# Preactivated 3x3 convolutions in float32: tiles of one size on TensorE, and row loads issued by ScalarE

## The chip, the cores and the metric

The kernel runs on one core of one Trainium2 chip. The metric is device time in microseconds of one execution, given as the median of several runs.

## The reference

The input `x` is 8 images of 8 channels of 1024 x 1024 float32 values. Two layers follow each other. Each normalises its input over groups of two channels (mean and variance over the group's two whole planes of one image), convolves the result 3x3 with 8 output channels and a padding of one, and adds the bias and the layer's own input.

```python
def _gn(v, G=4, eps=1e-5):
    B_, C_, H_, W_ = v.shape
    g = v.reshape(B_, G, C_ // G, H_, W_)
    m = jnp.mean(g, axis=(2, 3, 4), keepdims=True)
    s = jnp.var(g, axis=(2, 3, 4), keepdims=True)
    return ((g - m) / jnp.sqrt(s + eps)).reshape(v.shape)
...
x = x + _L0_conv_ref(_gn(x), L0_conv_weight, L0_conv_bias)
x = x + _L1_conv_ref(_gn(x), L1_conv_weight, L1_conv_bias)
```

## The kernel before

**Tiling.** The 128 partitions hold 16 image rows of 8 channels each (a block, 512 KB). An image has 64 blocks; two of them make a unit, so that a layer of an image (a pass) has 32 units and the kernel has 16 passes and 512 units. `x_tile` has 8 slots of one block, so four units' worth. The result of a unit is gathered in PSUM (`conv`, two parities of two blocks of 1024 columns, all of PSUM), evicted with the bias by ScalarE into `out_tile` (a ring of four units), and stored by GpSimd: layer 0 to the scratch tensor `mid_dram`, layer 1 to the output. Normalisation is folded into the weights `wts` (the rstd) and the bias, so that the matmuls read `x_tile` as it was loaded; the residual is an identity added to the middle tap.

**Matmuls of a unit.** The three kernel rows are one banded weight matrix over (row, channel), the three kernel columns are three shifts `kw` of the moving rows, and a unit has two halves `c` of 512 columns. A quarter is 32 partitions, four image rows. Its output needs its own rows and some of the quarter above. `whole` makes the odd quarters with four matmuls of 64 rows by 32 columns, `split` makes the even ones with eight matmuls of 32 by 32: the quarter's own rows (L405) and the quarter above (L410), the latter for the other half of the columns, `1 - c`. One `whole` and one `split` are called a round here; a unit has six, in the order of lines 424 to 437. The profile shows two records for each matmul call, since float32 goes through in two passes. After three rounds the wait at L431 asks for the end of the first half, because the second half adds to the same places of PSUM from other rows of the array.

**Order of the work.** SP issues all loads in one queue: the row blocks, and the 1 MB pieces of the next image that VectorE takes statistics of (`load_stat`, 32 for each image, at the units in `STAT_UNITS`). After the matmuls of unit g have ended (`conv_done`) it loads the second block of unit g+3 and the first of unit g+4. ScalarE evicts unit g in three activations. VectorE takes the statistics of `out_tile` in layer 0 (four instructions a unit) and of the next image's pieces. Between two passes VectorE, TensorE and ScalarE work out mean, variance, weights and bias (`sums_of`, `sums`); no matmul of the next pass can start before.

In the rows the matmuls are named by their lines: L395 `whole`, L405 and L410 `split`.

## Time and profile before

| | |
|---|---|
| median of 3 runs | 6538.94 us (6537.51 to 6539.03) |
| the profiled execution's own time | 6541.13 us |
| its span in the trace | 6539.5 us |
| TensorE busy | 6236.9 us (95%), mean granted clock 0.984 |
| ScalarE, VectorE, GpSimd busy | 1711.8, 1424.5, 591.4 us |
| moved by DMA | 1344.60 MB, 206 GB/s over the span |

The span is the time from the first to the last instruction. A share of busy time of TensorE says only that some matmul was in the array; up to sixteen tiles of 32 by 32 can be at work at once, and the share doesn't tell how many were. The granted clock is the part of TensorE's 2.4 GHz that it was given: 1.0 is 2.4 GHz, 0.5 is 1.2 GHz.

### The profile page before, as it was taken

Reading aid. Unit: us, or ns where it says so; the run is one execution under the profiler, and the core shown is the slowest. Engines: PE = TensorE matmul, PEld = TensorE weight load, DVE = VectorE, ACT = ScalarE, POOL = GpSimd, SP = SyncE. Lnnn points to the kernel's source line nnn. Section 1 sums busy time; section 2 is a strip of 40 time slices with the busy share of each in tenths; the row PEclk is TensorE's granted clock in tenths of the full one; section 3 lists DMA queues with packets and bytes.
Section 4 is the critical chain, followed back from the end, with each engine's and each line's share of the span. In section 5 each row is a group of like instructions: output and inputs, shape, how many; then the busy total and the mean of one; then the engine's idle time right before and its main releaser. Section 6 shows DMA issues by size and latency. Waiting matters only on the chain.

```text
span 6539.5 us, 167994 instructions
## 1 busy us (share of the span) xinstructions
PE 6236.9 (95%) x74176; PEld 1052.5 (16%) x74176; DVE 1424.5 (22%) x2460; ACT 1711.8 (26%) x1553; POOL 591.4 (9%) x1059
## 2 busy tenths in 40 slices
PE   2999999999999999999999999999999999999999
PEld 0111111111111111111111111111111111111111
DVE  6332113321133101331113311223012331022100
ACT  0222222222222222222222222222222222222222
POOL 0000010000000000000010000100000000000000
PEclk9999999999999999999999999999999999999999
DMA  7665666756566566766666666666666666655454
GB/s 273 219 215 203 218 191 216 226 202 215 191 218 225 199 214 193 217 205 214 223 186 219 205 221 209 200 215 204 219 206 203 213 206 217 207 162 177 154 172 153
DMA packets 334159, 1344.60 MB, mean 206 GB/s; under 512 B 38800, under 2 KB 38928, under 8 KB 301200
## 3 DMA queue, kind: packets, MB, share of 16 engines
q1 hardware_dynamic: 184688, 805.91, 40.8%
q0 software_dynamic: 147456, 536.94, 21.9%
q14 instruction: 186, 1.52, 0.1%
q10 hardware_dynamic: 1824, 0.14, 0.0%
q8 instruction: 5, 0.08, 0.0%
HBM read 805.45 MB, written 536.87 MB: 205 GB/s over the span
## 4 chain that ended last, share of the span: by engine, by line
PE 95%; DVE 2%; issue 1%; DMA 1%; ACT 1%; SPq 0%; DVEq 0%; ACTq 0%; POOL 0%; POOLq 0%
PE conv L395 47%; PE conv L405 45%; PE conv L410 3%; DMA stat_tile<-x_dram 1%; DVE bn_x L602 1%; DVE mv_mid L490 0%; ACT out_tile L344 0%; ACT out_tile L346 0%; DVE wts L541 0%; DVE bn_mid L476 0%; DVE newton L531 0%; DVE x_tile L556 0%; PE conv L371 0%; PE conv L367 0%; SPq L183 0%
## 5 line engine op out<-in xcount | busy, mean ns | idle before, releaser
L410 PE MATMUL conv<-x_tile,wts 32*32 32x512 f32 x24576 | 3334.1, 602 | 0.0
L405 PE MATMUL conv<-x_tile,wts 32*32 32x512 f32 x24576 | 3334.0, 602 | 0.0
L395 PE MATMUL conv<-x_tile,wts 64*32 64x512 f32 x24576 | 3281.4, 604 | 34.9 <-DVE bias L562 34.9
L342 ACT ACTIVATE out_tile<-conv,bias 128x1024 f32<-128x1024 f32 x512 | 570.6, 1114 | 4619.3 <-PE conv L410 4619.3
L476 DVE BATCH_NORM_STATS2 bn_mid<-out_tile 128x6 f32<-128x512 f32 x1024 | 658.7, 685 | 2241.6 <-ACT out_tile L342 1989.6
L468 DVE BATCH_NORM_STATS2 bn_x<-stat_tile 128x6 f32<-128x512 f32 x896 | 550.6, 679 | 2013.8 <-DMA stat_tile<-x_dram 2013.8
L405 PEld LDWEIGHTS conv<-x_tile,wts 32*32 32x32 f32 x24576 | 530.4, 103 | 2591.3 <-issue 2591.3
L395 PEld LDWEIGHTS conv<-x_tile,wts 64*32 64x32 f32 x24576 | 475.9, 105 | 2612.3 <-issue 2612.3
L346 ACT ACTIVATE out_tile<-conv,bias 64x1024 f32<-64x1024 f32 x512 | 569.3, 1112 | 13.1
L344 ACT ACTIVATE out_tile<-conv,bias 64x1024 f32<-64x1024 f32 x512 | 567.4, 1108 | 13.0
L297 POOL DMA_DIRECT2D mid_dram<-out_tile x512 | 273.8, 535 | 2845.6 <-ACT out_tile L342 2319.2
L297 POOL DMA_DIRECT2D out_dram<-out_tile x512 | 269.0, 525 | 2895.0 <-ACT out_tile L342 2425.9
L410 PEld LDWEIGHTS conv<-x_tile,wts 32*32 32x32 f32 x24576 | 530.4, 103 | 0.0
L367 PE MATMUL conv<-share,average 128*128 128x4 f32 x32 | 7.7, 311 | 183.4 <-DVE share L488 111.0
L497 DVE COPY mean<-conv 128x4 f32<-128x4 f32 x16 | 2.6, 163 | 394.3 <-PE conv L367 394.3
L602 DVE BATCH_NORM_STATS2 bn_x<-stat_tile 128x512 f32 x128 | 78.9, 681 | 24.1 <-DMA stat_tile<-x_dram 23.7
L377 PE MATMUL conv<-taken,plain 64*32 64x1 f32 x384 | 13.5, 190 | 58.0 <-DVE plain L539 58.0
L304 POOL TENSOR_SCALAR pad_row<-zeros,own_mean 8x1024 f32<-8x1024 f32 x16 | 46.0, 2873 | 150.7 <-DVE own_mean L525 120.0
L352 ACT ACTIVATE root<-var 128x4 f32<-128x4 f32 x16 | 3.3, 205 | 134.4 <-DVE var L517 134.3
L367 PEld LDWEIGHTS conv<-share,average 128*128 128x128 f32 x32 | 6.6, 256 | 196.3 <-issue 196.3
L483 DVE BATCH_NORM_AGGREGATE mv_x<-bn_x 128x2 f32<-128x192 f32 x32 | 29.3, 978 | 4.6 <-DVE bn_x L468 4.3
L490 DVE BATCH_NORM_AGGREGATE mv_mid<-bn_mid 128x2 f32<-128x768 f32 x8 | 29.0, 3622 | 1.2 <-DVE bn_mid L476 0.3
(48 smaller groups left out, 123.9 us busy)
## 6 DMA issues: line engine op xcount, KB each, us to landing
stat_tile<-x_dram SPq DMA_DIRECT2D x256, 1024.0 KB, 8.8
mid_dram<-out_tile POOLq DMA_DIRECT2D x512, 512.0 KB, 6.7
out_dram<-out_tile POOLq DMA_DIRECT2D x512, 512.0 KB, 5.3
x_tile<-x_dram SPq DMA_DIRECT2D x504, 512.0 KB, 6.0
x_tile<-mid_dram SPq DMA_DIRECT2D x504, 512.0 KB, 4.3
x_tile<-x_dram SPq DMA_DIRECT2D x8, 480.0 KB, 6.6
x_tile<-mid_dram SPq DMA_DIRECT2D x8, 480.0 KB, 6.4
x_tile<-pad_row SPq DMA_DIRECT2D x16, 32.0 KB
```

The source lines that it names most:

```text
L297: pool.dma_start(to, out_tile[:, g % RING, i]).then_inc(stored[g % RING], 16)
L304: pool.tensor_scalar(pad_row[0:CH, :], zeros[0:CH, :], own_mean[0:CH, 0:1], None, ALU.add).then_inc(pad_row_filled, 1)
L342: act.activation(out_tile[:, slot, 0], conv[:, parity, 0], ACT.Identity, bias=bias[:, 0:1]).then_inc(evicted, 1)
L344: act.activation(out_tile[HALF:P, slot, 1], conv[0:HALF, parity, 1], ACT.Identity, bias=bias[0:HALF, 0:1]).then_inc(evicted, 1)
L346: act.activation(out_tile[0:HALF, slot, 1], conv[HALF:P, parity, 1], ACT.Identity, bias=bias[HALF:P, 0:1]).then_inc(evicted, 1)
L395: nc.tensor.matmul(columns_of(parity, i, 2 * h + 1, c), wts[part, WHOLE, kw], rows_of(HALF * h, HALF, 2 * j + i, c, kw), start=(kw == 0), ...
L405: nc.tensor.matmul(columns_of(parity, i, 2 * h, c), wts[part, SPLIT, kw], rows_of(HALF * h, TILE, slot, c, kw), start=first, stop=end)
L410: last = nc.tensor.matmul(columns_of(parity, i, 2 * h, 1 - c), wts[part, SPLIT, kw], rows_of(TILE * q, TILE, above, 1 - c, kw), start=firs ...
L468: last = dve.bn_stats(bn_x[:, i * STAT_PARTS + q, :], stat_tile[:, s, q * BANK:(q + 1) * BANK])
L476: last = dve.bn_stats(bn_mid[:, (2 * u + i) * HALVES + h, :], out_tile[:, u % RING, i, h * BANK:(h + 1) * BANK])
L483: last = dve.bn_aggr(mv_x[:, g, :], bn_x[:, g * PER_GROUP:(g + 1) * PER_GROUP, :] .rearrange("p a b -> p (a b)"))
L602: last = dve.bn_stats(bn_x[:, bass.ds(k * (STAT_SLOTS * STAT_PARTS) + (s * STAT_PARTS + q), 1), :] .rearrange("p a b -> p (a b)"), stat_ti ...
```

## The change

`whole` and `split` are replaced by one function `add`, in which every matmul has 32 rows by 32 columns: for each of the two blocks of a unit, four for the quarters' own rows (MAIN) and four for the quarters above (ABOVE). A unit has 96 matmul calls in place of 72. The wait on `half_added` stands between the third and the fourth round. The bias matmuls (`sums`) are 24 in place of 12, and the weights, the identity and the table of taps have the forms MAIN and ABOVE.

The row blocks, the pad row and the head row are issued by ScalarE, in `load_next(n, g)` behind the three activations of unit g; the conditions are the same, except that the head row of layer 1 is asked for at unit 4 in place of unit 0. SP keeps the statistics pieces alone; in its loop it waits for the matmuls of the unit before the one at which a piece is due, and for a free slot of `stat_tile`. At the start, ScalarE asks for the first seven blocks behind its table of taps.

```diff
-            def whole(parity, j, c, kw):
-                for i in range(2):
-                    for h in range(2):
-                        part = slice(HALF * h, HALF * (h + 1))
-                        nc.tensor.matmul(columns_of(parity, i, 2 * h + 1, c), wts[part, WHOLE, kw],
-                                         rows_of(HALF * h, HALF, 2 * j + i, c, kw),
-                                         start=(kw == 0), stop=(kw == KW - 1))
-
-            def split(parity, j, c, kw):
+            def add(parity, j, c, kw):
                 first, end = c == 0 and kw == 0, c == 1 and kw == KW - 1
                 for i in range(2):
                     slot = 2 * j + i
-                    for h in range(2):
-                        part = slice(HALF * h, HALF * h + TILE)
-                        nc.tensor.matmul(columns_of(parity, i, 2 * h, c), wts[part, SPLIT, kw],
-                                         rows_of(HALF * h, TILE, slot, c, kw), start=first, stop=end)
-                        q = 1 if h else 3
+                    for q in range(QUARTERS):
                         part = slice(TILE * q, TILE * (q + 1))
-                        above = slot if h else (slot - 1) % SLOTS
-                        last = nc.tensor.matmul(columns_of(parity, i, 2 * h, 1 - c),
-                                                wts[part, SPLIT, kw],
-                                                rows_of(TILE * q, TILE, above, 1 - c, kw),
+                        nc.tensor.matmul(columns_of(parity, i, q, c), wts[part, MAIN, kw],
+                                         rows_of(TILE * q, TILE, slot, c, kw), start=first, stop=end)
+                    for q in range(QUARTERS):
+                        above = (q - 1) % QUARTERS
+                        part = slice(TILE * above, TILE * (above + 1))
+                        last = nc.tensor.matmul(columns_of(parity, i, q, 1 - c), wts[part, ABOVE, kw],
+                                                rows_of(TILE * above, TILE,
+                                                        slot if q else (slot - 1) % SLOTS, 1 - c, kw),
                                                 start=first, stop=end)
                 return last
...
-                whole(parity, j, 0, 0)
-                split(parity, j, 0, 0)
-                whole(parity, j, 0, 1)
-                split(parity, j, 0, 1)
-                whole(parity, j, 0, 2)
-                split(parity, j, 0, 2).then_inc(half_added, 1)
-                whole(parity, j, 1, 0)
+                for kw in range(KW):
+                    last = add(parity, j, 0, kw)
+                last.then_inc(half_added, 1)
                 pe.wait_ge(half_added, UNITS * p + TRIP * t + (j + 1))
                 pe.sem_inc(unit_begun)
-                split(parity, j, 1, 0)
-                whole(parity, j, 1, 1)
-                split(parity, j, 1, 1)
-                whole(parity, j, 1, 2)
-                last = split(parity, j, 1, 2)
+                for kw in range(KW):
+                    last = add(parity, j, 1, kw)
                 last.then_inc(conv_done, 1)
...
+            def load_next(n, g, last_image):
+                layer, u = divmod(g, UNITS)
+                if g == UNITS:
+                    for s in range(RING):
+                        act.wait_ge(stored[s], stores_before(n, UNITS + s))
+                        act.sem_inc(rows_asked)
...
+                if layer == 0 and u == RING:
+                    act.wait_ge(stored[0], stores_before(n, RING))
+                    act.sem_inc(rows_asked)
+                    load_head(1, n)
...
+                if (g + TRIP - 1) % UNITS == UNITS - 1:
+                    load_last_pad(layer, n)
+                    load(TRIP, 0)
+                    act.wait_ge(last_pad_loaded, 32 * n + 16 * (layer + 1))
+                    act.sem_inc(rows_asked)
+                    load(TRIP - 1, 1)
+                else:
+                    load(TRIP - 1, 1)
+                    load(TRIP, 0)
...
                                bias=bias[HALF:P, 0:1]).then_inc(evicted, 1)
-
-            def image(n, first_image):
+                load_next(n, g, last_image)
...
-            def image(n, last_image):
-                for g in range(2 * UNITS):
...
+            def image(n):
+                for i in range(STATS):
+
+                    sp.wait_ge(conv_done, units_through(n, STAT_UNITS[i] - 1) if STAT_UNITS[i] else
+                               2 * UNITS * n + 1)
                     sp.sem_inc(rows_wanted)
+                    load_stat(n + 1, i, STATS * n + (STATS + i + 1 - STAT_SLOTS))
```

On TensorE, the start of a unit read before like this (the matmuls of the first round and of half the second):

```order
L395 MATMUL conv<-x_tile,wts 32x512 x4
L405 MATMUL conv<-x_tile,wts 32x512
L410 MATMUL conv<-x_tile,wts 32x512
L405 MATMUL conv<-x_tile,wts 32x512
L410 MATMUL conv<-x_tile,wts 32x512
L405 MATMUL conv<-x_tile,wts 32x512
L410 MATMUL conv<-x_tile,wts 32x512
L405 MATMUL conv<-x_tile,wts 32x512
L410 MATMUL conv<-x_tile,wts 32x512
L395 MATMUL conv<-x_tile,wts 32x512 x4
```

And now, from the second round of a unit to the wait in its middle (here L390 is MAIN and L395 is ABOVE):

```order
L390 MATMUL conv<-x_tile,wts 32x512 x4
L395 MATMUL conv<-x_tile,wts 32x512 x4
L390 MATMUL conv<-x_tile,wts 32x512 x4
L395 MATMUL conv<-x_tile,wts 32x512 x4
L412 REGISTER_ALU
L390 MATMUL conv<-x_tile,wts 32x512 [waits half_added]
L390 MATMUL conv<-x_tile,wts 32x512 x3
L395 MATMUL conv<-x_tile,wts 32x512 x4
```

The tiles of 64 rows are gone, and the wait has a whole round of 32 by 32 matmuls ahead of it whose end it needs; before, the four matmuls of a `whole` stood between.

On ScalarE two evictions in the middle of layer 0 read before:

```order
L342 ACTIVATE out_tile<-conv,bias 128x1024 [waits mid_taken,stored1,conv_done]
L344 ACTIVATE out_tile<-conv,bias 64x1024
L346 ACTIVATE out_tile<-conv,bias 64x1024
L342 ACTIVATE out_tile<-conv,bias 128x1024 [waits mid_taken,stored2,conv_done]
L344 ACTIVATE out_tile<-conv,bias 64x1024
L346 ACTIVATE out_tile<-conv,bias 64x1024
```

And now, at unit 28 of layer 0, where the pad row is asked for as well:

```order
L329 ACTIVATE out_tile<-conv,bias 128x1024 [waits mid_taken,stored0,conv_done]
L331 ACTIVATE out_tile<-conv,bias 64x1024
L333 ACTIVATE out_tile<-conv,bias 64x1024
L282 DMA x_tile<-pad_row 8x1024 [waits stored0,stored1,stored2,stored3,pad_row_filled]
L273 DMA x_tile<-mid_dram 128x1024
L273 DMA x_tile<-x_dram 120x1x1024 [waits last_pad_loaded]
L329 ACTIVATE out_tile<-conv,bias 128x1024 [waits mid_taken,stored1,conv_done]
L331 ACTIVATE out_tile<-conv,bias 64x1024
L333 ACTIVATE out_tile<-conv,bias 64x1024
L273 DMA x_tile<-mid_dram 128x1024 x2
```

Each eviction is followed by two loads, and at unit 28 the next eviction stands behind a wait for the pad row's landing.

## Rows read from the trace of the kernel before

**Rows 1.** The page: the span, and TensorE's busy time.

```profile
span 6539.5 us, 167994 instructions
...
PE 6236.9 (95%) x74176; PEld 1052.5 (16%) x74176; DVE 1424.5 (22%) x2460; ACT 1711.8 (26%) x1553; POOL 591.4 (9%) x1059
```

**Rows 2.** The page: the chain that ended last, by line.

```profile
PE conv L395 47%; PE conv L405 45%; PE conv L410 3%; DMA stat_tile<-x_dram 1%; DVE bn_x L602 1%; DVE mv_mid L490 0%; ACT out_tile L344 0%; ACT out_tile L346 0%; DVE wts L541 0%; DVE bn_mid L476 0%; DVE newton L531 0%; DVE x_tile L556 0%; PE conv L371 0%; PE conv L367 0%; SPq L183 0%
```

**Rows 3.** Timeline, one round: start, duration (us), engine, line, instructions.

```profile
3011.06 1.06 PE L395 MATMUL conv<-x_tile,wts 64*32 64x512 f32 x8
...
3012.05 0.10 PEld L405 LDWEIGHTS conv<-x_tile,wts 32*32 32x32 f32 x1 [0.84 <-issue]
3012.05 0.61 PE L405 MATMUL conv<-x_tile,wts 32*32 32x512 f32 x1
...
3012.51 0.59 PE L405 MATMUL conv<-x_tile,wts 32*32 32x512 f32 x1
...
3012.55 0.59 PE L410 MATMUL conv<-x_tile,wts 32*32 32x512 f32 x1
3013.07 0.15 PEld L395 LDWEIGHTS conv<-x_tile,wts 64*32 64x32 f32 x8 [0.84 <-issue]
```

**Rows 4.** Waits: who waited for what, us in total, times, longest.

```profile
PEld conv L395 <- issue: 2612.3, 3072, 2.6
PEld conv L405 <- issue: 2591.3, 3072, 1.7
```

**Rows 5.** Timeline of ScalarE, one eviction and the next one's start.

```profile
3019.28 1.11 ACT L342 ACTIVATE out_tile<-conv,bias 128x1024 f32<-128x1024 f32 x1 [8.68 <-PE conv L410]
...
3021.55 1.11 ACT L346 ACTIVATE out_tile<-conv,bias 64x1024 f32<-64x1024 f32 x1
3031.35 1.11 ACT L342 ACTIVATE out_tile<-conv,bias 128x1024 f32<-128x1024 f32 x1 [8.68 <-PE conv L410]
```

**Rows 6.** The page: DMA queues (q1 SP, q0 GpSimd): packets, MB, share.

```profile
q1 hardware_dynamic: 184688, 805.91, 40.8%
q0 software_dynamic: 147456, 536.94, 21.9%
```

**Rows 7.** Windows: busy us by engine, then granted clock, DMA share, GB/s.

```profile
82.00:92.00 10.00, 0.00 (x0) 0.00 (x0) 2.38 (x4) 0.00 (x0) 0.00 (x0) 1.00 1.04 242
110.00:150.00 40.00, 32.38 (x368) 6.65 (x370) 10.80 (x31) 6.88 (x7) 4.75 (x4) 1.00 0.24 68
516.00:528.00 12.00, 4.21 (x44) 2.23 (x52) 9.73 (x30) 0.20 (x1) 2.90 (x1) 0.50 0.23 93
546.00:550.00 4.00, 4.00 (x56) 0.67 (x48) 0.00 (x0) 0.00 (x0) 0.00 (x0) 1.00 1.00 405
948.00:956.00 8.00, 8.00 (x112) 1.33 (x96) 2.57 (x4) 3.33 (x3) 1.07 (x2) 1.00 0.97 256
```

**Rows 8.** The issue line of the row loads: duration ns min/median/max, and landing.

```profile
L183 SPq DMA_DIRECT2D x_tile<-x_dram x512: 536/540/970, 73.5 to 6090.2; - x171
L183 SPq DMA_DIRECT2D x_tile<-mid_dram x512: 327/333/438, 473.5 to 6495.8; - x171
...
DMA to landing us min/median/max: 3.2/4.7/19.6
```

**Rows 9.** Timeline of TensorE around the end of layer 0 of image 0.

```profile
505.90 1.06 PE L395 MATMUL conv<-x_tile,wts 64*32 64x512 f32 x8
...
525.75 1.93 PE L395 MATMUL conv<-x_tile,wts 64*32 64x512 f32 x8 [2.51 <-DVE bias L562]
...
529.49 1.08 PE L395 MATMUL conv<-x_tile,wts 64*32 64x512 f32 x4
```

**Rows 10.** Timeline of ScalarE at the end of image 0.

```profile
914.21 1.11 ACT L342 ACTIVATE out_tile<-conv,bias 128x1024 f32<-128x1024 f32 x1 [8.68 <-PE conv L410]
```

**Rows 11.** Timeline of TensorE at the start of image 1.

```profile
922.48 1.93 PE L395 MATMUL conv<-x_tile,wts 64*32 64x512 f32 x8 [1.78 <-DVE bias L562]
```

More of the change, by code:

```diff
@@ L37 @@
 PASSES = 2 * IMAGES
-WHOLE, SPLIT = range(2)
+MAIN, ABOVE = range(2)
+QUARTERS = P // TILE
 HALVES = SIDE // BANK
@@ new lines, in rows_of, with load_block @@
+            def rows_of(layer, n, first, rows):
+                if layer == 0:
+                    return x_by_row[first:first + rows, bass.ds(n, 1)].rearrange("r n c w -> r (n c) w")
+                return mid[bass.ds(n, 1), CH * first:CH * (first + rows), :] \
+                    .rearrange("n a w -> (n a) w")
+            def load_block(layer, n, b):
+                first = ROWS * b + 1
+                rows = ROWS - 1 if b == BLOCKS - 1 else ROWS
+                act.dma_start(x_tile[0:CH * rows, b % SLOTS, 1:SIDE + 1],
+                             rows_of(layer, n, first, rows)).then_inc(rows_loaded[b % SLOTS], 16)
@@ L354, in image @@
                     for u in range(UNITS):
-                        evict(n, layer * UNITS + u, first_image)
-            image(0, True)
-            with act.Fori(1, IMAGES) as n:
-                image(n, False)
+                        evict(n, layer * UNITS + u, first_image, last_image)
+            load_head(0, 0)
+            for b in range(LAST_SLOT):
+                load_block(0, 0, b)
+            image(0, first_image=True)
+            with act.Fori(1, IMAGES - 1) as n:
+                image(n)
+            image(IMAGES - 1, last_image=True)
         @block.tensor
@@ L374, in sums @@
                 pe.sem_inc(unit_begun)
-                for j in range(P // TILE):
-                    for kw in range(KW):
-                        last = nc.tensor.matmul(
-                            conv[TILE * j:TILE * (j + 1), 0, 0, GROUPS:GROUPS + 1],
-                            plain[0:HALF, kw], taken[0:HALF, :],
-                            start=(kw == 0), stop=(kw == KW - 1))
+                for j in range(QUARTERS):
+                    for kind in (MAIN, ABOVE):
+                        for kw in range(KW):
+                            last = nc.tensor.matmul(
+                                conv[TILE * j:TILE * (j + 1), 0, 0, GROUPS:GROUPS + 1],
+                                plain[0:TILE, kind, kw], taken[0:TILE, :],
+                                start=(kind == MAIN and kw == 0), stop=(kind == ABOVE and kw == KW - 1))
                 last.then_inc(bias_summed, 1)
@@ L538, in make_weights @@
                 wait_for_all()
[L539 removed]
+                dve.tensor_scalar(plain[:, :, :, :], band[:, layer], own_rstd[:, 0:1], None,
                                   ALU.mult).then_inc(taken_known, 1)
```

122 lines of the change are left out of this document (38 added, 84 removed).

## The prediction

> **What bounds the kernel now.** I read the page first: TensorE has a matmul in flight for 6236.9 of 6539.5 us [rows 1], and the chain that ended last is its conv matmuls for 95% [rows 2]. So the time is TensorE's, but a busy share doesn't say how full the array was. For that I took the timeline of one round [rows 3]. Eight records of `whole` start at 3011.06 and run 1.06 us. The first of `split` starts at 3012.05, when they are through, and the next `whole` at 3013.07: a round takes 2.01 us, 0.99 for `whole` and 1.02 for `split`, one behind the other. Inside `split` eight matmuls of different tiles start together, and the second pass of each 0.46 us after the first (3012.05, 3012.51). By `columns_of`, `whole` writes column quarters 1 and 3 from all 128 rows, `split` quarters 0 and 2 from all rows: the two halves of a round use different halves of the array and still don't overlap. What the reader is to see is the idle time of the weight loads: 0.84 us ahead of each `whole` and of each `split` [rows 3], 3072 times each, that is six times in each of 512 units, 2612.3 and 2591.3 us in all [rows 4]. Within a kind the weights are loaded while other matmuls run; across the kinds nothing is loaded ahead, though the tiles wanted are free. A unit takes six rounds, 12.07 us from one eviction to the next [rows 5]; 512 of them are 6180 us, and the other 360 us are the start (some 118 us: of 110 to 150 TensorE is busy for 32.38 [rows 7]) and the changes of pass.
>
> The second reading is of DMA, since it comes next. The two queues' packets take 40.8% and 21.9% of 16 engines' span [rows 6]: 62.7% of 6539.5 us are **4100 us of transfers** if the engines never idled. At a full share the rate depends on what is moved: 242 GB/s for rows of `x_dram` alone, whose pieces of 4 KB lie 4 MB apart from channel to channel, 256 in a mixed stretch of layer 0 and 405 in one of layer 1 [rows 7]. 4100 us correspond to 327 GB/s for the page's 1344.60 MB, between these.
>
> **The change, part by part.**
>
> *Rounds of sixteen tiles.* A round is now 16 calls of 32 by 32 that cover the array exactly once (`columns_of`: block i, quarter q, own rows in column quarter q+2i, rows above the same), with no other kind between. If the sixteen run as the eight of `split` do, a round costs its two passes, 2 x 0.46 = 0.92 us, with the next weights loaded behind them. Six are 5.5 us. The wait for `half_added` was covered by the four matmuls of a `whole`; now the array must empty ahead of it. No row shows that; its lower bound is nothing, its upper bound one pass, 0.46 us, and I take 0.3, for the load of 0.10 us and the 0.13 to 0.15 us by which a matmul of 0.59 to 0.61 us outlasts its pass [rows 3]. **A unit is 5.8 us** on TensorE, 2970 us for 512. The profile of before has nothing with more than eight tiles at once, so two steps are open: that the kinds were what kept the halves apart, and that the array takes sixteen streams, four in each row quarter, where it took two.
>
> The Trainium skill says the first outright (TensorEngine Tiling (Array Packing), section Key Properties): changing the tiling mode, not merely the tile, drains TensorE. The idle 0.84 us of the weight loads agree [rows 3]. By the rule a round falls to 0.92 us; without it the next limit below would leave it at 1.84.
>
> *ScalarE issues the row loads.* An issue takes 0.54 us for a block of x and 0.33 for one of mid on SP [rows 8], two a unit, so 0.7 to 1.1 us on top of the evictions, which take 3.4 us (3019.28 to 3022.66, three of 1.11 [rows 5]): 4.1 to 4.5 us a unit, under 5.8. The loads go out behind the eviction, 3.4 us later than before. The block that is wanted soonest is the second of unit g+3: the cycle from the end of unit g to the end of unit g+3 is 3.4 (eviction) + 0.5 (issue) + landing + 5.8 (matmuls), over three units. With the median landing of 4.7 us [rows 8] that is 4.8 us a unit, under TensorE's 5.8; it comes to the 7.8 us below only when a landing takes 13.7. Behind the issues the next eviction is queued, and behind it the stores and the matmuls two units on; that has 5.8 + 5.8 - 4.5 us of room. Cost: nothing while DMA is the bound.
>
> *SP keeps the statistics.* Its megabyte no longer stands ahead of rows in one ring; the bytes are the same. VectorE's work a unit is unchanged and no bound: 1424.5 us in all [rows 1]. The 12 extra bias matmuls of a pass (records of some 0.05 us) and the larger `plain` are under 1 us, 16 times: 10 us.
>
> *What binds next.* TensorE wants a unit every 5.8 us, DMA delivers one every 4000/512 = 7.8 (4100 less about 100 at the start). So TensorE waits some 2 us a unit for rows and **DMA is the bound**. The gaps may cost it its clock: in the change of layer the granted clock was 0.50, 1.2 GHz [rows 7], after its last round had ended at 507.9 (505.90 and 2.01), and the first round after it took 3.74 us (525.75 to 529.49) in place of 2.01 [rows 9]. One such cold round adds 1.7 us, and 5.8 + 1.7 = 7.5 is still under 7.8: the waiting absorbs it.
>
> *Where DMA will idle.* In the first 150 us: between 110 and 150 the share was 0.24 [rows 7], so 30 us idle; with a unit shorter by 6 us, 24. At a change of layer TensorE restarts 17.8 us after its last round (507.9 to 525.75 [rows 9]), its first unit takes 7.5 and the eviction 3.4, so loads go out again after 28.7 us. What is queued at the moment of the stop lasts some 10 us (a landing of 13.7 less the 3.9 since the last issue) and the last eviction adds 2 MB, 6.4 us: idle 12. At a change of image the restart comes after 8.3 us (914.2 to 922.48 [rows 10, 11]): idle 8.3 + 7.5 + 3.4 - 16.4, about 3. Eight of each: 120 us. At units 28 of each pass ScalarE waits for the pad row behind its own queue, up to 10 us; I take 4 us of it 16 times, 64. The last eviction and store: 9.
>
> *Sum.* 4100 + 24 + 120 + 64 + 9 + 10 = 4327. Packets of three queues that are never empty will take somewhat longer than in a mix with pauses: 242 GB/s of x rows alone at a full share against 327 on average says the direction, no row says how much; between nothing and 12% I take 2%, 85 us. That gives 4412 us of span, 1.6 us more for the execution (6541.13 against 6539.5). The profiled execution lies 0.03% over the median of the runs: **4415 us**. Own range: 4050 (the transfers overlap some per cent better than their sum) to 4900 (12% longer).
>
> **The rivals.**
>
> *Rows come too late (about 5300 us).* ScalarE's queue shares the engines with two others, and each load lands as late as the latest did, 19.6 us [rows 8]. Then a unit takes (9.7 + 19.6)/3 = 9.8 us, 5000 in all, with start and changes 5300. For it: the loads leave 3.9 us later and the pad's wait stalls ScalarE. Against: a long landing is itself a full DMA, and then the sum above holds. Chance 0.09.
>
> *Eight tiles at once is what the array gives (about 6150 us).* Sixteen take turns, 1.84 us a round, 6 x 1.84 + 0.3 = 11.3 us a unit, 0.77 x 512 = 390 us less than now. For it: no row shows more than eight. Against: idle weight loads, which a full array wouldn't explain. Chance 0.07.
>
> *The wait in the middle decides (about 6690 us, slower).* The rounds stay at 2.01 us, for whatever reason, and `half_added` has lost its cover: 0.3 x 512 = 154 us more. It turns slower once a round saves less than 0.05 us. For it: 96 calls in place of 72. Against: sixteen starts at the spacing of `split`'s eight (within 0.05 us) are 0.1 us, far below a pass. Chance 0.06, and 0.01 that it comes out even.
>
> *Row quarters take turns in a bank (about 11700 us).* In a round now four row quarters write to different columns of one bank at once. If they took turns, a round would be 4 x 0.92 us and a unit 22.4. But `split` already has two quarters in one bank, rows 0 and 64 by L405, and all eight start within 0.05 us [rows 3]. Chance 0.01. The Trainium skill states such a rule (PSUM — Partial Sum Buffer, PSUM bank collisions raise a hardware error): different row tiles can't access one bank at the same time. The trace doesn't agree.
>
> *DMA runs at its best rate throughout (about 3600 us).* 405 GB/s [rows 7] for all 1344.60 MB are 3320 us and the idle time 280. Against: 242 for x rows. Chance 0.03.
>
> **How the numbers follow.** DMA-bound: 0.73. The range 4050 to 5400 holds nearly all of it and the first rival, 0.80. Faster by over 0.2% (what a measurement here can tell from no change): 0.73 + 0.09 + 0.07 + 0.03 = 0.92; within 0.2%: 0.01; slower: 0.06 + 0.01 = 0.07.
>
> **What would show it.** In the timeline of after, sixteen first passes should start within about 0.1 us, rounds should follow each other by 0.92 us with no idle weight load between, and about 0.3 us of gap should stand in the middle of a unit. ScalarE's evictions should be 7 to 8.5 us apart, longer in layer 0; the DMA share 0.9 or more; the chain should go over loads into `x_tile`; TensorE should wait for them. Wrong it would be if rounds take 1.8 us or more, or if the DMA share stays under 0.8 while TensorE waits for rows, which is the late queue.

## The result, and the profile after

The changed kernel takes 3968.06 us (median of 4 runs, 3966.73 to 3969.04) against 6538.98 beside it on the same chip: a ratio of 0.607 [0.606, 0.608], 39% less. The forecast was 4415 us with a range of 4050 to 5400, so the time came out 447 us under the forecast and 82 us under the range.

The page of the changed kernel: span, busy time by engine, DMA in all, and the queues with packets, MB and share (q10 is ScalarE's, q0 GpSimd's, q1 SP's):

```profile
span 3965.1 us, 217004 instructions
...
PE 3489.6 (88%) x99136; PEld 1836.0 (46%) x99136; DVE 1430.5 (36%) x2460; ACT 1710.2 (43%) x1553; POOL 590.8 (15%) x1061
...
q10 hardware_dynamic: 149648, 537.60, 39.3%
q0 software_dynamic: 147456, 536.94, 34.5%
q1 hardware_dynamic: 36864, 268.45, 18.8%
```

The other engines' busy times are those of before [rows 1]; TensorE's fell by 2747 us, while that of its weight loads (PEld) rose from 1052.5 to 1836.0. The queues' shares add up to 92.6% where they were 62.7% [rows 6]. At first sight DMA is the bound, as forecast. The waits (who waited for what, us in total, times, longest) say something else:

```profile
ACT out_tile L329 <- PE conv L395: 1947.6, 497, 15.8
PEld conv L390 <- issue: 1424.6, 3152, 7.8
...
PE conv L390 <- DMA x_tile<-x_dram: 67.9, 53, 6.9
```

TensorE waited for rows 53 times, 67.9 us, where the forecast has about 2 us in each of 512 units; ScalarE waited for TensorE 1947.6 us. The last bound is still TensorE. Its timeline from the middle of a unit (460.15) over its end (463.43) to the middle of the next (466.98), and on to the middle of the one after it (473.70), some groups of each round:

```profile
460.15 0.63 PE L390 MATMUL conv<-x_tile,wts 32*32 32x512 f32 x4
...
460.24 0.63 PE L395 MATMUL conv<-x_tile,wts 32*32 32x512 f32 x4
460.58 0.63 PE L390 MATMUL conv<-x_tile,wts 32*32 32x512 f32 x4
...
461.00 0.85 PE L390 MATMUL conv<-x_tile,wts 32*32 32x512 f32 x4
461.26 0.66 PE L395 MATMUL conv<-x_tile,wts 32*32 32x512 f32 x4
...
461.86 0.59 PE L390 MATMUL conv<-x_tile,wts 32*32 32x512 f32 x1
...
462.08 0.83 PE L390 MATMUL conv<-x_tile,wts 32*32 32x512 f32 x4
...
463.43 0.63 PE L390 MATMUL conv<-x_tile,wts 32*32 32x512 f32 x4
...
465.36 0.84 PE L390 MATMUL conv<-x_tile,wts 32*32 32x512 f32 x4
...
466.98 0.63 PE L390 MATMUL conv<-x_tile,wts 32*32 32x512 f32 x4
...
469.98 0.80 PE L390 MATMUL conv<-x_tile,wts 32*32 32x512 f32 x4
...
473.70 0.63 PE L390 MATMUL conv<-x_tile,wts 32*32 32x512 f32 x4
```

Sixteen matmuls start within 0.11 us (in groups of four, from 460.15 to 460.24), their second passes at 460.58, and the next round at 461.00: 0.85 us for a round that took 2.01 [rows 3]. That is the forecast's round. The next does not start so: one matmul is there at 461.00, the other three of its group start from 461.20 on (a narrower window shows it), the other groups from 461.26 on, and the round lasts 1.08 us (461.00 to 462.08; one matmul of the third round is ahead of the others, at 461.86). Both halves read like this here: 0.85, 1.08, and 1.08 with a gap behind it: 0.27 us at the end of a unit (462.08 to 463.43 is 1.35) and 0.54 in its middle, where `half_added` is waited for (465.36 to 466.98 is 1.62). A unit is 2 x (0.85 + 1.08 + 1.08) + 0.54 + 0.27 = 6.83 us here. In 300 of the 496 units that another of the same pass follows there is no gap at the end: the next unit's first round then stands 3.0 us behind the middle (466.98 to 469.98) and follows a round like the rest, and from middle to middle it is 6.72 us (466.98 to 473.70). The weight loads show where the 0.23 us between 0.85 and 1.08 lie:

```profile
460.58 0.10 PEld L390 LDWEIGHTS conv<-x_tile,wts 32*32 32x32 f32 x1 [0.19 <-issue]
...
461.01 0.35 PEld L390 LDWEIGHTS conv<-x_tile,wts 32*32 32x32 f32 x6 [0.33 <-issue]
...
461.26 0.10 PEld L395 LDWEIGHTS conv<-x_tile,wts 32*32 32x32 f32 x1
```

At the start of the second round (461.00) most of its weights aren't there; the next groups of matmuls start when their loads come, from 461.26 on. What these loads wait for the trace doesn't name. ScalarE's timeline shows the unit, and its DMA issues (ACTq) beside its activations:

```profile
463.58 1.11 ACT L329 ACTIVATE out_tile<-conv,bias 128x1024 f32<-128x1024 f32 x1 [3.34 <-PE conv L395]
463.59 1.09 ACTq L273 DMA_DIRECT2D x_tile<-mid_dram  x2
...
470.41 1.11 ACT L329 ACTIVATE out_tile<-conv,bias 128x1024 f32<-128x1024 f32 x1 [3.45 <-PE conv L395]
...
477.13 1.11 ACT L329 ACTIVATE out_tile<-conv,bias 128x1024 f32<-128x1024 f32 x1 [3.34 <-PE conv L395]
```

Evictions are 6.83 and 6.72 us apart. I took the starts of all 512 from the timeline, for a sum of the span: the first stands at 134.3 us, 496 steps inside passes take 3454 us (median 6.72, mean 6.96), 15 steps across a change of pass 367 us (24.5 each), and 10 us follow the last. Before, the same four are 134.1, 5983 (12.06 each), 413 (27.5 each) and 10. The gain is in the units, 2529 us, and 46 us in the changes. What the mean has over the median lies in layer 0 (mean 7.19; 6.74 in layer 1), and there not in image 7, beside which no statistics are loaded: its 31 steps of layer 0 are at most 6.83 us. In the code the two loads stand behind three activations. In the trace they are issued 0.01 us after the first activation has started. The windows (busy us by engine, granted clock, DMA share, GB/s) of layer 0, layer 1 and the change of layer between:

```profile
200.00:220.00 20.00, 19.55 (x592) 10.42 (x574) 11.81 (x19) 10.00 (x9) 3.19 (x6) 1.00 1.03 396
400.00:420.00 20.00, 19.55 (x592) 10.53 (x575) 2.76 (x5) 9.99 (x9) 3.14 (x6) 1.00 1.02 419
360.00:380.00 20.00, 5.47 (x128) 3.96 (x125) 13.27 (x30) 3.54 (x4) 4.01 (x3) 0.63 0.45 163
```

DMA shows a full share in both layers and TensorE is busy for 19.55 of 20 us in both. A share of 1.03 stands beside 396 GB/s here and beside 242 in [rows 7]: it doesn't tell how much more DMA could carry.

### The profile page after: what moved, and what is told of

It is laid out like the page before. It is cut to its first block and busy times, and to the rows that moved or that the text cites. A ratio compares the mean times of both kernels' runs of the same rounds, so it can differ in the third digit from the quotient of the medians.

```text
span 3965.1 us, 217004 instructions
## 1 busy us (share of the span) xinstructions
PE 3489.6 (88%) x99136; PEld 1836.0 (46%) x99136; DVE 1430.5 (36%) x2460; ACT 1710.2 (43%) x1553; POOL 590.8 (15%) x1061
## 3 DMA queue, kind: packets, MB, share of 16 engines
q10 hardware_dynamic: 149648, 537.60, 39.3%
## 5 line engine op out<-in xcount | busy, mean ns | idle before, releaser
L390 PE MATMUL conv<-x_tile,wts 32*32 32x512 f32 x49152 | 3398.7, 603 | 173.0 <-DMA x_tile<-x_dram 67.9
L395 PE MATMUL conv<-x_tile,wts 32*32 32x512 f32 x49152 | 3421.9, 606 | 2.5 <-issue 2.5
L390 PEld LDWEIGHTS conv<-x_tile,wts 32*32 32x32 f32 x49152 | 1597.1, 103 | 1734.2 <-issue 1424.6
L329 ACT ACTIVATE out_tile<-conv,bias 128x1024 f32<-128x1024 f32 x512 | 570.2, 1114 | 2016.4 <-PE conv L395 1947.6
L395 PEld LDWEIGHTS conv<-x_tile,wts 32*32 32x32 f32 x49152 | 956.8, 103 | 79.3 <-issue 4.6
L370 PE MATMUL conv<-taken,plain 32*32 32x1 f32 x768 | 34.0, 188 | 85.1 <-DVE plain L517 85.1
L370 PEld LDWEIGHTS conv<-taken,plain 32*32 32x32 f32 x768 | 33.1, 149 | 86.0 <-issue 86.0
```

The lines of the kernel that those rows point to most:

```text
L329: act.activation(out_tile[:, slot, 0], conv[:, parity, 0], ACT.Identity, bias=bias[:, 0:1]).then_inc(evicted, 1)
L370: last = nc.tensor.matmul(conv[TILE * j:TILE * (j + 1), 0, 0, GROUPS:GROUPS + 1], plain[0:TILE, kind, kw], taken[0:TILE, :], start=(kind = ...
L390: nc.tensor.matmul(columns_of(parity, i, q, c), wts[part, MAIN, kw], rows_of(TILE * q, TILE, slot, c, kw), start=first, stop=end)
L395: last = nc.tensor.matmul(columns_of(parity, i, q, 1 - c), wts[part, ABOVE, kw], rows_of(TILE * above, TILE, slot if q else (slot - 1) % S ...
```

## The experiments

All ratios are to the kernel before, run beside each on the same chip.

### The two parts of the change alone

*Squares, rows by SP.* The change's TensorE part with the loads where they were:

```diff
-                act.dma_start(x_tile[0:CH * rows, b % SLOTS, 1:SIDE + 1], ...
+                sp.dma_start(x_tile[0:CH * rows, b % SLOTS, 1:SIDE + 1], ...
...
-                load_next(n, g, last_image)
```

> Half of the change alone: TensorE works in squares of 32, but SP issues the row loads as before, in one queue with the statistics pieces. Theory A (the squares bring the gain, TensorE is the bound of the changed kernel with some 6.7 us a unit, and who issues the loads hardly matters): 3950 to 4050 us. Theory B (transfers run at over 385 GB/s only because rows, statistics and stores lie in three queues): rows alone and rows behind a 1 MB piece run at 242 to 330 GB/s again, 4250 us or more.

Measured: 4020.96 us, 0.615 [0.614, 0.616].

*Old tiles, rows by ScalarE.* The kernel before with `load_next` behind its evictions, and SP with the statistics alone.

> The other half alone: tiles of 64 by 32 and 32 by 32 as before, row loads issued by ScalarE. Theory A: TensorE's unit stays at 12.07 us and covers everything, 6530 to 6550 us. Theory B says the same here. A third: issues on ScalarE delay evictions by 0.7 to 1.1 us a unit, which shows only at the 16 changes of pass, under 20 us.

Measured: 6571.32 us against 6540.02, 1.005 [1.003, 1.007], which is more than the 20 us that the third reading allowed. So the squares alone bring 2519 us. The move to ScalarE costs 31 us with the old tiles: the steps inside passes are what they were (5983 us), the changes of pass take 439 us in place of 413 and the first eviction is 4 us later. With the squares it saves 53: the steps inside passes take 3527 us with the rows on SP and 3454 with the rows on ScalarE, the changes 348 and 367, and the first eviction stands at 126.5 and 134.3 us. The loss is at the start and at the changes of image, with either kind of tiles (22.3 and 26.1 us each with the old ones, 18.9 and 21.7 with the squares); the changes of layer stay as they are (32.1 and 26.9). The gain inside the passes is all in layer 0 (1855 to 1782 us; layer 1 takes 1673 and 1672), where rows are late.

### What DMA can carry

*Two rounds of six.* TensorE's work cut to a third, all bytes kept:

```diff
-                for kw in range(KW):
-                    last = add(parity, j, 0, kw)
+                last = add(parity, j, 0, 0)
                 last.then_inc(half_added, 1)
...
-                for kw in range(KW):
-                    last = add(parity, j, 1, kw)
+                last = add(parity, j, 1, KW - 1)
```

> The changed kernel with two rounds of a unit in place of six (one kernel column in each half, so two thirds of the convolution is left out); all loads, stores, evictions and waits stay. TensorE then needs some 2.4 us a unit, and the transfers or ScalarE's 4.5 us must show. Theory A (the changed kernel is bound by TensorE, and the DMA engines have room over 390 GB/s): clearly below, 3500 to 3750 us. Theory C (the changed kernel is bound by DMA, the share of 1.02 means what it says): 3900 to 3970 us, as the changed kernel. By the sum of the prediction (packets need as long as they did before, 4100 us) it would be 4300.

Measured: 3566.04 us, 0.545 [0.544, 0.546]. The windows of layer 0 and layer 1, and TensorE's waits:

```profile
160.00:320.00 160.00, 89.62 (x1536) 15.41 (x1536) 88.75 (x142) 77.10 (x70) 24.98 (x47) 0.63 1.02 403
370.00:520.00 150.00, 87.74 (x1504) 14.66 (x1489) 29.66 (x48) 77.84 (x71) 24.19 (x47) 0.61 1.02 420
...
PE conv L390 <- DMA x_tile<-x_dram: 444.3, 161, 11.5
PE conv L390 <- DMA x_tile<-mid_dram: 389.8, 164, 7.1
```

Here TensorE does wait for rows, 834 us, and for evictions another 412. The same megabytes that the prediction counted as 4100 us of transfers go through in 3566, idle times and start included. This is the run that the forecast fell by.

*A quarter of the statistics' bytes.* The pieces of images 1 to 7 load 512 of 2048 columns; the statistics then are of old data in part.

```diff
+                if used is not None and not isinstance(n, int):
+                    sp.dma_start(stat_tile[:, s, 0:BANK],
+                                 x_rows[bass.ds((n * STATS + i) * STAT_ROWS, P), 0:BANK]) \
+                      .then_inc(stat_loaded[s], 16)
+                    return
```

> The changed kernel with the statistics pieces of images 1 to 7 loaded to a quarter (256 KB in place of 1 MB; VectorE reads what lies in the rest, so the statistics of these images are not the right ones). 176 MB of 1344 are gone. Theory A (TensorE is the bound): 3850 to 3970 us, only the waits for rows (68 us in all) and part of the changes of pass can go. Theory C (DMA is the bound): 13% fewer bytes, 3480 to 3600 us.

Measured: 3865.25 us, 0.591 [0.590, 0.592]: 13% fewer bytes (1168.16 MB), 2.6% less time, 103 us. A bound by bytes would have given some 500. By the eviction starts all of it comes from inside the passes: 3355 us in place of 3454, a mean step of 6.76 for 6.96 at the same median of 6.72, with the changes and the start as they were. TensorE then waits 2.3 us for rows. So DMA costs the change 98 us by rows that come late, 0.2 us a unit, and hardly more; a step of 6.72 is TensorE's own. Of the 98, 59 are in the last three steps of the passes, where the wait for the pad row stands (below). The queues' share, by the page, is 91.2% with 13% fewer bytes, where it was 92.6%: it hardly follows the bytes.

*The same two rounds with the rows issued by SP*, so that rows and statistics share a queue again:

> Two rounds in place of six as in the earlier run, but SP issues the row loads in one queue with the statistics pieces. Theory B (three queues keep the transfers at their rate): 3566 us rises by 8% or more, to over 3850. Theory A (the engines care little who issues): under 3680 us.

```profile
160.00:320.00 160.00, 75.64 (x1392) 13.68 (x1379) 82.53 (x132) 72.52 (x66) 23.38 (x44) 0.64 1.02 361
370.00:520.00 150.00, 80.10 (x1536) 15.19 (x1536) 34.28 (x56) 76.66 (x69) 24.11 (x46) 0.70 0.97 395
```

Measured: 3722.95 us, 0.569 [0.568, 0.570], 157 more than with ScalarE's queue and between the two theories, at the same DMA share of 1.02 in layer 0. With three queues it is 403 GB/s, with two 361. The Trainium skill (DMA: Bandwidth & Descriptors, section Issuing engines are not separate DMA queues) says that issuing from several engines saves only the issuing time. Here the measurement differs: SP's queue stood waiting for TensorE's matmuls for 2413.5 of its 3715 us, so that it had time to issue, and the share in layer 0 was full in both. The run doesn't separate the number of queues from the order in them, though: on SP a block stands behind a megabyte piece and behind that piece's wait for a free slot of `stat_tile`, which held the queue 27 times, 65.8 us in all.

*And with the rows of `x` taken contiguously* (from the wrong places, so that the data are others; the bytes are the same and their pieces still 4 KB, but they lie one behind the other in place of 4 MB apart):

```diff
-                    return x_by_row[first:first + rows, bass.ds(n, 1)].rearrange("r n c w -> r (n c) w")
+                    return x.rearrange("n c h w -> n (c h) w")[0:1, CH * first:CH * (first + rows), :] \
+                        .rearrange("n a w -> (n a) w")
```

> Two rounds in place of six, ScalarE issues, and the rows of x are read as one contiguous piece (of image 0 for every image, so the data are not the right ones) in place of pieces of 4 KB that lie 4 MB apart. Theory P (the distance costs only where rows of x move alone, as at 82 to 92 us of the kernel before with 242 GB/s, and is hidden beside other queues' transfers): within 1.5% of 3566 us. Rival (it costs in a mix too): 3300 to 3450 us.

```profile
160.00:320.00 160.00, 85.06 (x1491) 14.63 (x1472) 90.29 (x145) 80.00 (x72) 25.50 (x48) 0.62 1.02 415
370.00:520.00 150.00, 85.75 (x1536) 15.12 (x1536) 31.02 (x49) 76.18 (x70) 24.05 (x46) 0.67 1.01 415
```

Measured: 3493.89 us, 0.534 [0.533, 0.535]. Layer 0 goes from 403 to 415 GB/s, the time down by 72 us, 2%, a little more than theory P allowed and less than the rival asked for. The 242 GB/s that rows of `x` show when they go alone [rows 7] is no rate that they impose on a mix.

### What holds the tiles

Two runs add one matmul of a single column of zeros after each round but the last; they differ only in its size, 64 rows or 32:

```diff
+                if not end:
+                    last = nc.tensor.matmul(conv[0:TILE, parity, 0, c * BANK:c * BANK + 1], zeros[0:HALF, 0:TILE],
+                                            zeros[0:HALF, 0:1], start=False, stop=False)
```

> The changed kernel with one tiny matmul more behind each round but a unit's last: 64 rows by 32 columns, one moving column, weights and data of zeros, added to one column of the sum. Theory M (what kept the halves of a round apart was the change between 64 by 32 and 32 by 32): the array empties ahead of each and behind each, as in the kernel before, 0.4 to 0.8 us a round, five a unit: 5000 to 6000 us. Theory O (a matmul only waits for the tiles that it needs): two tiles are held for some 0.1 us each, the same time as the next run, 4000 to 4350 us.

> The same tiny matmul with 32 rows, so that no tile size changes. Theories M and O both: one tile is held for some 0.1 us, 5 a unit, 4000 to 4350 us. The difference to the run with 64 rows is the price of the size alone.

With 64 rows (the last group of a round, the tiny one, the next round):

```profile
519.85 0.61 PE L395 MATMUL conv<-x_tile,wts 32*32 32x512 f32 x4
520.39 0.22 PE L400 MATMUL conv<-zeros 64*32 64x1 f32 x2
520.77 0.63 PE L390 MATMUL conv<-x_tile,wts 32*32 32x512 f32 x4 [0.17 <-PE conv L400]
```

With 32 rows:

```profile
520.14 0.64 PE L390 MATMUL conv<-x_tile,wts 32*32 32x512 f32 x4
...
520.22 0.16 PE L400 MATMUL conv<-zeros 32*32 32x1 f32 x1
...
520.43 0.86 PE L390 MATMUL conv<-x_tile,wts 32*32 32x512 f32 x4
```

The matmul of 64 rows starts 0.54 us after the round's last group, when that is nearly through (520.46); the next round waits for it in turn. That of 32 rows starts while the round's second passes are running, and the next round follows 0.21 us behind. The median step inside a pass is 7.56 us with the first and 6.81 with the second, against 6.72: 0.84 us for five visits of another size, 0.09 for five of the same. This is the rule that the prediction took from the Trainium skill (TensorEngine Tiling (Array Packing), section Key Properties), and the trace agrees.

The totals must not be used: 5381.31 us, 0.823 [0.821, 0.825], with 64 rows and 4896.12 with 32 (two runs, 4814.38 and 4977.87, too far apart for a ratio). The first lies in theory M's range by luck, the second outside what both theories gave. 512 units at their medians would be 430 and 46 us more than the change, not 1413 and 928. The difference shows in the pages, in the queue by which TensorE fetches its instructions (q8: packets, MB, share) and TensorE's waits; in the change it is 6 packets:

```profile
q8 instruction: 610, 9.99, 0.8%
...
PE conv L390 <- issue: 499.9, 189, 7.4
```

That is the kernel with 64 rows; with 32 it is 511 packets and 496.8 us. The longer body of the loop over trips is fetched again and again. The waits are about half of what is missing. Beside them the clock is lower. In one such step of 21.1 us in the kernel with 32 rows TensorE stands for 7.21 us ahead of 1041.12, and the granted clock of the stretch is 0.67, where it was 1.00 in an undisturbed one before it; how much of the rest this makes was not measured:

```profile
1013.00:1020.00 7.00, 6.83 (x224) 3.54 (x203) 2.47 (x4) 3.33 (x3) 1.05 (x2) 1.00 0.97 387
1034.00:1055.00 21.00, 12.27 (x219) 4.00 (x235) 2.47 (x4) 3.28 (x3) 1.05 (x2) 0.67 0.57 211
```

### What a round and a wait cost

*Blocks side by side.* `add` goes over the two blocks inside the loop over the quarters, so that no two neighbours use the same column quarter:

```diff
-                for i in range(2):
-                    slot = 2 * j + i
-                    for q in range(QUARTERS):
+                for q in range(QUARTERS):
+                    for i in range(2):
+                        slot = 2 * j + i
```

> The changed kernel with the 16 matmuls of a round in another order: for each quarter own rows and rows above of both blocks, in place of all four quarters' own rows, then all four above. Theory L (rounds two and three of a half take 1.08 us and not 0.85 because the weight loads are taken in order, and one whose tile is still busy holds up those behind it): the order decides how much is held up, so the time moves by over 1% in one of the directions. Rival (each tile simply needs its time): within 0.3% of 3968 us.

Measured: 3966.01 us, 0.606 [0.605, 0.607]: no difference to 3968.06, where theory L asked for over 1%. The order within a round doesn't matter, so a load held up by the busy tile of another ahead of it is not shown to be what makes 1.08 of 0.85.

*A wait between all rounds.*

```diff
+                    if kw < KW - 1:
+                        last.then_inc(round_done, 1)
+                        pe.wait_ge(round_done, 4 * (UNITS * p + TRIP * t) + (4 * j + kw + 1))
+                        pe.sem_inc(unit_begun)
```

> The changed kernel with a wait for the round's own end behind every round, so five waits inside a unit in place of one. If a wait costs the 0.3 us that the prediction took for the one on half_added, four more are 1.2 us a unit and 4450 to 4600 us. Theory L: a round that starts on an empty array needs 0.85 us and not 1.08, which gives most of the drain back, so under 0.2 us a wait, 4100 to 4350 us.

Measured: 4618.22 us, 0.706 [0.705, 0.708], just above the first range and far from theory L's. Four waits more a unit: (4618.2 - 3968.1) / (4 x 512) = 0.32 us each; by the median unit, 8.21 against 6.72, it is 0.37, and the difference is that no row is late any more at this pace (mean step 8.23). A round with a wait behind it stands 1.43 us ahead of the next (519.10 to 520.53). This is what a wait adds on balance: a gap of 0.58, less the 0.23 by which the round behind it is shorter, since all sixteen start at once again:

```profile
519.10 0.63 PE L391 MATMUL conv<-x_tile,wts 32*32 32x512 f32 x4 [0.16 <-PE conv L396]
...
520.53 0.63 PE L391 MATMUL conv<-x_tile,wts 32*32 32x512 f32 x4 [0.28 <-PE conv L396]
```

*Half the columns.* Four of the six rounds write 256 columns of each 512, all bytes kept:

```diff
-                return x_tile[first:first + rows, slot, at:at + BANK]
+                return x_tile[first:first + rows, slot, at:at + (BANK if kw == 0 else BANK // 2)]
```

> The changed kernel with half the moving columns (256 in place of 512) in rounds two and three of each half unit, so a third of the convolution's adding is left out. In the changed kernel a round on an empty array takes 0.85 us, rounds two and three 1.08, which is what the prediction's 0.92 missed. Theory L (0.23 us a round are weight loads that can't go ahead, whatever the columns): rounds two to three follow by 0.43 + 0.23 = 0.66 us. Theory D (64 instructions a round come at a fixed pace of 17 ns): still 1.08 us. Rival (the pass itself is longer when sixteen tiles run): 0.54 us, half of 1.08. By L and the last the time falls to the transfers' 3566 to 3700 us, by D it stays at 3900 or more.

```profile
463.43 0.64 PE L391 MATMUL conv<-x_tile,wts 32*32 32x256 f32 x5
463.69 0.45 PE L396 MATMUL conv<-x_tile,wts 32*32 32x256 f32 x4
...
464.12 0.57 PE L391 MATMUL conv<-x_tile,wts 32*32 32x256 f32 x4
464.32 0.45 PE L396 MATMUL conv<-x_tile,wts 32*32 32x256 f32 x4
```

A round of 256 columns takes 0.63 to 0.69 us here (463.69 to 464.32, 463.43 to 464.12). Halving the columns takes two halved passes off, 0.42 us of the 0.85 of a round that isn't held, and 0.42 from 1.08 is 0.66. So some 0.23 us of a following round don't shrink with its columns. That theory L names the reason, the weight loads, is not shown by this: behind a wait all 32 loads of a round begin within 0.17 us (460.12 to 460.29) and hold up nothing, so it isn't their length, and what holds them in the other rounds stays open. The reading by which nothing of a round scales (1.08) is out, and that by which all of it does (0.54) doesn't fit these rounds. The total, 3817.41 us, 0.584 [0.583, 0.585], lies above the 3566 to 3700 expected, since TensorE now waits 238.5 us for rows of `x`, 164.7 for rows of `mid_dram`, and for evictions.

### The pad row

At unit 28 of a pass ScalarE waits for the pad row. ScalarE's timeline in the changed kernel, at the end of layer 0 of image 0:

```profile
332.78 0.73 ACTq L282 DMA_DIRECT2D x_tile<-pad_row  x1
...
342.22 0.95 ACTq L273 DMA_DIRECT2D x_tile<-x_dram  x1
343.30 1.11 ACT L329 ACTIVATE out_tile<-conv,bias 128x1024 f32<-128x1024 f32 x1 [7.56 <-issue]
```

ScalarE is idle for 7.56 us ahead of this eviction, which starts 10.94 us behind the one before it (332.36) in place of 6.72, and TensorE stands 6.33 us ahead of 352.66, for a block of `x_dram`, as the one asked for at 342.22 is. It happens at the end of layer 0 in images 0 to 6 (7.56 to 8.16 us): the last three steps of these passes take 28.1 to 29.8 us, and 20.1 in every layer 1 and in layer 0 of image 7, beside which no statistics are loaded. So the wait costs something only where DMA is late as well. Two ways without it:

*The wait on TensorE*, in the pass's last trip, written out behind the loop:

```diff
+                if last_trip and j == TRIP - 1:
+                    pe.wait_ge(last_pad_loaded, 16 * p + 16)
...
-                    load(TRIP, 0)
-                    act.wait_ge(last_pad_loaded, 32 * n + 16 * (layer + 1))
-                    act.sem_inc(rows_asked)
-                    load(TRIP - 1, 1)
```

> The same removal in another way: TensorE waits for the pad in the last trip, which is taken out of the loop, so that its code is twice as long. If only the stall counts, the time is that of the run above, 3850 to 3910 us. If longer code of TensorE has to be fetched again, as the two runs with the tiny matmul seem to show (8 to 10 MB on the instruction queue in place of 0.1), it is slower than that by 100 us or more.

Measured: 4109.93 us, 0.628 [0.627, 0.629], 142 us slower than the change. TensorE's code is longer by a trip, its instruction queue has 222 packets, and it waited 107.8 us for issue ahead of L385. By the eviction starts the longest steps of a pass are those to the third unit of the trip written out and to the third unit of the loop's first trip: 11.49 and 12.12 us in the mean.

*No wait at all*: the last slot is always loaded in two pieces, fifteen rows and one, so that the pad piece never overlaps the block and TensorE waits for both on `rows_loaded`:

```diff
+                rows = ROWS - 1 if b % SLOTS == LAST_SLOT else ROWS
...
+                if b % SLOTS == LAST_SLOT and b < BLOCKS - 1:
+                    act.dma_start(x_tile[P - CH:P, LAST_SLOT, 1:SIDE + 1],
+                                  rows_of(layer, n, first + rows, 1)) \
+                       .then_inc(rows_loaded[LAST_SLOT], 16)
```

> The changed kernel without ScalarE's wait for the pad row: the last slot's block comes in two transfers (15 rows, and the row of the last 8 partitions, which at the end of a layer is the pad), both counted by the slot's own semaphore, so nobody waits for the pad by itself. In the changed kernel that wait holds the eviction of unit 29 for 7.6 us at the end of layer 0 and TensorE then waits 6.3 us for the last block. If this stall is what the waits for rows of x are (67.9 us in 53), 3968 falls by 60 to 120 us: 3850 to 3910. If DMA is late there by itself, it stays within 20 us.

Measured: 3943.11 us, 0.603 [0.602, 0.604]. Since that is 0.6% from the change, both ran again, side by side, five times each:

> The changed kernel again, as the base of the next run: 3960 to 3975 us.

> The version in which nobody waits for the pad row by itself, beside the changed kernel on one chip. If its 25 us are real, it is faster by 0.4 to 0.8%; if they were the chip's, within 0.2%.

Measured: the change 3971.11 us (3959.94 to 3976.69), 0.6075 [0.6066, 0.6083]; two pieces 3944.76 (3942.19 to 3951.14), 0.6036 [0.6027, 0.6044]. The intervals don't meet: the version without the wait is 26 us faster, the fastest here that computes all. The expected 60 to 120 us were too many. The eviction starts show why it is no more. The last three steps inside a pass take 384 us in the change, over 16 passes, and 328 here: 56 saved. The 28 ahead of them take 3069 and 3105: 36 given back. In layer 0 every fourth step is longer there (up to 8.39 us in the mean over the images, 6.98 in the change). Why rows come later there was not tried: the two pieces are only 784 packets more on q10 (150432 for 149648), and a pause in the loads that let DMA catch up would do it too, which is argued and not shown.

## Why the prediction was wrong

**The step that failed** is the second reading: "62.7% of 6539.5 us are 4100 us of transfers if the engines never idled". It took the time that packets were under way as work that keeps its size. In the changed kernel the same megabytes take 92.6% of 3965.1 us, 3672 us, and with TensorE cut short they fit into 3566. With a quarter of the statistics, 13% fewer bytes, it is 91.2% of 3865.2 us, 3525. So the packets' time is no fixed price of the bytes; what it holds besides them was not measured. From the failed step came 7.8 us a unit, "DMA is the bound", and the low end of 4050. [Rows 7] held the hint: a share of 1.04 beside 242 GB/s and of 1.00 beside 405. The prediction read that as a rate that depends on what is moved, kept the average, and on top of it added 2% for a busier mix, where the sign was the other. The rival that took the best rate throughout, 3600, with a chance of 0.03, lies near what DMA needs when TensorE's work is cut (3566 measured), but is not the kernel's time, because of the next term.

**A unit of 5.8 us on TensorE** was mis-sized: 6.72. A round on an empty array takes 0.85 us (0.92 forecast), but "with the next weights loaded behind them" fails for those that follow another, 1.08 each. The six rounds of the unit at 460 are 6.02 us in place of 5.5, its gap in the middle 0.54 in place of 0.3, and the 0.27 at its end was left out; that gap is there in 196 of 496 units, always at the end of a trip of four, and for what, the trace doesn't say. With the measured unit the times add up, though not from rows of before: 496 x 6.76 (as with a quarter of the statistics) is 3353, the start, changes and end of before 134 + 413 + 10, together 3910; late rows add 98, the shorter changes take off 46, which makes 3962 for a span of 3965. The two errors have opposite signs: with DMA's limit right and a unit of 5.8 us still in the sum, the forecast would have been some 3570 to 3600, under the time by more than 360. That 4415 came no further off is in part luck. (Its last step is rounded up by some 3 us: 4412 and 1.6, less 0.03%, are 4412.)

**Right** was what the squares do: tiles of one size let sixteen matmuls start together (within 0.11 us; "about 0.1" was asked for), eight tiles are not the array's limit, and row quarters share a bank without turns. ScalarE's issues cost nothing inside the passes (the steps of layer 1 are the same 1672 us), and less than thought, since "3.4 us later than before" is 0.01 us after the eviction's start. Of what was to show it, the DMA share of 0.9 came true for a wrong reason: it would have been 0.9 under TensorE as a bound as well, so it tells nothing between the two. TensorE's 67.9 us of waits for rows do.

**The pad's wait** was put at 64 us, 4 us in each of 16 passes. In its own place it costs 56, in seven passes of the 16, with ScalarE idle for 7.6 to 8.2 us (up to 10 was forecast); the units ahead of it give 36 back, and the medians differ by 26. That the 64 came near the 56 is luck.

**The move of the loads**, "nothing while DMA is the bound", is a gain of 53 us with the squares, and the runs that DMA bounds show the same sign, 157 us. That issues cost nothing at the changes fails too: 26 us with the old tiles, 19 with the squares. **The changes of pass** were to leave DMA idle for 120 us on top of its 4100; with TensorE as the bound what counts is their length, 24.5 us in place of 27.5.

## What to carry to other kernels

Don't turn a DMA busy share into microseconds of work: ask what rate the same bytes reached in a full window, and if DMA may bind next, take TensorE's work out of the kernel, keep the bytes, and time that. Two limits that lie 400 us apart still meet: late rows cost 98 us here, though DMA's own limit was 10% below the time. And when matmuls of sixteen tiles replace larger ones, don't take a round from its two passes alone: one that follows another takes 0.23 us more here, before its weights are loaded.

## What the runs showed of the hardware

- The DMA share stands at 1.02 to 1.04 for 242, 361, 403 and 420 GB/s.
- With the row loads in a third queue the same transfers went at 403 GB/s in place of 361 in layer 0 and at 420 in place of 395 in layer 1 (share 1.02 in place of 0.97 there); the order within the queues changed with it.
- A DMA that stands behind three activations in ScalarE's code is issued 0.01 us after the first of them starts (463.59). For a block of `x` the issue takes 0.55 us in the median but up to 8.78 (the issue line, in ns: min, median, max), where SP's longest was 0.97 [rows 8]:

```profile
L273 ACTq DMA_DIRECT2D x_tile<-x_dram x512: 543/547/8782, 42.4 to 3703.1; - x171
```

- The length of TensorE's loop body has a price with a step in it: 6 packets of instructions in the change, 511 with 5 more matmul calls a unit, with 500 us of waiting and a granted clock of 0.67 around such a wait. The Trainium skill (Runtime: NRT & Kernel Launch, section Instruction fetch mechanics) calls the cost of a long stream mostly hidden and warns of branches to code that has left the window; the runs agree with the second, in a loop.
- In the windows of the runs with two rounds a unit TensorE's granted clock was 0.61 to 0.70, and rows still came late: 3566 us with 834 us of waits for them.
